# Two graph attention layers: both normalisations and the ELU's minimum on VectorE, half of the maxima subtracted inside the exponent, and a new order on every engine

## The reference

```python
q, k, v = x @ Wq + bq, x @ Wk + bk, x @ Wv + bv          # layer 0, 6 heads
probs = softmax(q @ k.T / sqrt(64) + where(adj, 0, NEG))
x = layernorm(x + (probs @ v) @ Wf + bf)
h = einsum('bnd,ade->bane', x, W)                        # layer 1, 12 heads
attn = tanh(h) @ w_src + (tanh(h) @ w_dst).T
attn = softmax(where(adj, leaky_relu(attn, 0.2), -999))
f = elu(attn @ h + b)
gate = sigmoid(x @ H_w.T + H_b)
out = layernorm(x + gate * f + (1 - gate) * x)
```

## Time and profile before

| | |
|---|---|
| median of 3 runs | 1220.42 us (1217.51 to 1220.64) |
| profiled execution | 1217.34 us, its span 1215.6 us |
| granted TensorE clock, mean | 0.974 |
| busy | PE 90%, PEld 80%, DVE 79%, ACT 80%, POOL 82% of the span |
| DMA engines | 31.2% |

### The profile page before, as it was taken

One profiled execution on the slowest core, in us unless ns is written; L12 is line 12 of the kernel. 1 busy time (PEld: TensorE's weight loads), 2 busy tenths in 40 slices (PEclk: granted clock), 3 DMA queues, 4 the chain that ended last, 5 costly groups with the idle time before them and its releaser, 6 DMA issues.

```text
span 1215.6 us, 35318 instructions
## 1 busy us (share of the span) xinstructions
PE 1091.1 (90%) x12234; PEld 975.3 (80%) x12297; DVE 962.6 (79%) x1948; ACT 968.6 (80%) x1868; POOL 1000.1 (82%) x813
## 2 busy tenths in 40 slices
PE   4689999999999999999999999999999999999851
PEld 4578888888888888888888888888888888888741
DVE  5567888888888888888888888888888888888843
ACT  5258888888888888888888888888888888888854
POOL 1138898888989888889988888988888898988876
PEclk9799999999999999999999999999999999999975
DMA  4103332223333222333322233332223333223233
GB/s 144 43 17 83 81 90 65 73 68 93 87 86 92 66 68 67 93 87 87 93 66 66 68 93 89 85 93 66 66 74 87 93 87 86 73 67 75 68 66 79
DMA packets 244762, 95.18 MB, mean 78 GB/s; under 512 B 223349, under 2 KB 239738, under 8 KB 244730
## 3 DMA queue, kind: packets, MB, share of 16 engines
q1 hardware_dynamic: 244730, 94.76, 31.2%
HBM read 31.22 MB, written 12.58 MB: 36 GB/s over the span
## 4 chain that ended last, share of the span: by engine, by line
PE 56%; POOL 15%; issue 14%; DVE 11%; ACT 2%; DMA 1%; DVEq 1%; SPq 0%; POOLq 0%; ACTq 0%
PE lin L448 33%; PE zp L545 6%; POOL z L1295 5%; POOL prod L1254 5%; PE fp L570 3%; PE zp L603 3%; PE zp L607 3%; DVE sd L978 2%; PE fp L620 2%; PE fp L573 2%; PE tp L487 2%; DVE y L1073 1%; DVE f L1117 1%; DVE z L1098 1%; ACT th L721 1%
## 5 line engine op out<-in xcount | busy, mean ns | idle before, releaser
L1302 POOL TENSOR_TENSOR p_lo<-z,p_hi 128x1536 f16<-128x1536 f32 x64 | 200.9, 3139 | 0.0
L1295 POOL TENSOR_TENSOR z<-z,z_max 128x1536 f32<-128x1536 f32 x64 | 176.5, 2758 | 9.1 <-DVE z_max L1105 6.1
L784 ACT ACTIVATE z<-zp 128x1536 f32<-128x1536 f32 x64 | 93.1, 1455 | 85.9 <-PE zp L607 85.9
L1254 POOL TENSOR_TENSOR prod<-th,w_sd_rows 128x768 f32<-128x768 f32 x64 | 120.5, 1883 | 14.0 <-ACT th L721 14.0
L620 PE MATMUL fp<-h_part,p1t_hi 128*128 128x33 bf16 x2304 | 110.6, 178 | 19.2 <-DMA p1t_lo<-p_lo 14.8
L620 PEld LDWEIGHTS fp<-h_part,p1t_hi 128*128 128x128 f16 x2304 | 104.4, 96 | 27.2 <-issue 24.1
L1307 POOL TENSOR_TENSOR f<-f,x_kept 128x384 f32<-128x384 f32 x64 | 64.7, 1011 | 73.6 <-DVE f L1124 69.4
L1098 DVE SCALAR_TENSOR_TENSOR z<-zp,z 128x1536 f32<-128x1536 f32 x64 | 112.2, 1753 | 11.0 <-ACT z L784 8.3
L776 ACT ACTIVATE p<-p,p_min 128x128 f32<-128x128 f32 x384 | 118.9, 396 | 0.0
L1105 DVE TENSOR_REDUCE z_max<-z 128x12 f32<-128x1536 f32 x64 | 111.6, 1744 | 0.0
L623 PE MATMUL fp<-h_part,p1t_lo 128*128 128x33 bf16 x1536 | 106.8, 178 | 0.0
(11 more groups left out here) (161 smaller groups left out, 4387.0 us busy)
## 6 DMA issues: line engine op xcount, KB each, us to landing
xt_raw<-x_t SPq DMA_DIRECT2D x32, 384.0 KB, 3.4
x_raw<-x SPq DMA_DIRECT2D x32, 384.0 KB, 3.5
out<-out_tile SPq DMA_DIRECT2D x64, 192.0 KB, 1.9
adj<-adj SPq DMA_DIRECT2D x64, 32.0 KB, 2.8
dst_row<-sd_t SPq DMA_DIRECT2D x64, 9.0 KB
p1t_hi<-p_hi SPq DMA_TRANSPOSE x64, 3.3
p1t_lo<-p_lo SPq DMA_TRANSPOSE x64, 3.3
z<-Wq SPq DMA_DIRECT2D x1, 576.0 KB, 3.5
```

The lines of the kernel that those rows point to most:

```text
L784: act.activation(z[:, g, :], zp[:, :, :].rearrange("p b n -> p (b n)"), ACT.Copy)\
L1254: pool.tensor_tensor(prod[:, g, :].rearrange("p (s d) -> p s d", s=2), th[:, g:g + 1, :].to_broadcast([128, 2, D]), rows["w_sd"][:, :].rea ...
L1295: pool.tensor_tensor(zs, zs, z_max[:, g, :].unsqueeze(2).to_broadcast([128, H1, N]), ALU.subtract)\
L1302: pool.tensor_tensor(p1_lo[:, g, :], z[:, g, :], p1_hi[:, g, :], ALU.subtract).then_inc(w1_lo[g].sem, 1)
```

## The change

Four things, and with them new orders on all five engines:
- The two normalisations move from ScalarE to VectorE, as one tensor_scalar each, (y - mean) x rstd; the two shifts go.
- The ELU's Relu on ScalarE becomes min(f, 1) on VectorE; the exponent takes the bias -1.
- GpSimd subtracts the maxima of heads 0 to 5 alone. For heads 6 to 11 VectorE makes an offset log(PSCALE) - max (`z_shift`, 12 columns), and ScalarE takes one exponent per head with that offset as the bias.
- The lists of steps are new, and with them the users' order of the PSUM banks `tp` and `fp`.

```diff
+SUBTRACTED = 6
...
-                def norm0(g):
-                    act.wait_ge(norm0_shift[g].sem, now(norm0_shift[g]))
...
-                    act.activation(x1[:, g, :], y[:, g, :], ACT.Identity, bias=shift0[:, g, :], scale=rstd[:, g, :])\
-                        .then_inc(x1_ready[g].sem, 1)
                 def z_exponent(g):
+                    act.wait_ge(z_offsets[g].sem, now(z_offsets[g]))
+                    for h in range(SUBTRACTED, H1):
+                        act.activation(z[:, g, N * h:N * (h + 1)], z[:, g, N * h:N * (h + 1)], ACT.Exp,
+                                       bias=z_offset[:, g, h:h + 1])
                     act.wait_ge(z_sub[g].sem, now(z_sub[g]))
-                    act.activation(z[:, g, :], z[:, g, :], ACT.Exp, bias=log_scale[:, :]).then_inc(z_exp[g].sem, 1)
+                    act.activation(z[:, g, 0:SUBTRACTED * N], z[:, g, 0:SUBTRACTED * N], ACT.Exp, bias=log_scale[:, :])\
+                        .then_inc(z_exp[g].sem, 1)
...
-                def shift_norm0(g):
+                def norm0(g):
                     dve.wait_ge(y_rstd[g].sem, now(y_rstd[g]))
...
+                    dve.wait_ge(x1t_mm[g].sem, now(x1t_mm[g]))
+                    dve.wait_ge(x1_copied[g].sem, now(x1_copied[g]))
+                    dve.tensor_scalar(x1[:, g, :], y[:, g, :], moments[:, g, 0:1], rstd[:, g, :],
+                                      ALU.subtract, ALU.mult).then_inc(x1_ready[g].sem, 1)
...
+                def z_shift(g):
+                    dve.wait_ge(z_maxed[g].sem, now(z_maxed[g]))
+
+                    dve.wait_ge(z_exp[g].sem, prev(z_exp[g]))
+                    dve.tensor_scalar(z_offset[:, g, :], z_max[:, g, :], -1.0, math.log(PSCALE), ALU.mult, ALU.add)\
+                        .then_inc(z_offsets[g].sem, 1)
...
+                def features_negative(g):
+
+                    dve.wait_ge(f_norm[g].sem, now(f_norm[g]))
+                    dve.wait_ge(f_elu[g].sem, prev(f_elu[g]))
+                    dve.tensor_scalar(f_neg[:, g, :], f[:, g, :], 1.0, None, ALU.min).then_inc(f_min[g].sem, 1)
...
-                def shift_norm1(g):
+                def norm1(g):
...
+                    dve.tensor_scalar(out_tile[:, g, :], y2[:, g, :], moments2[:, g, 0:1], rstd2[:, g, :],
+                                      ALU.subtract, ALU.mult).then_inc(out_ready[g].sem, 1)
...
-                    zs = z[:, g, :].rearrange("p (a n) -> p a n", a=H1)
+                    zs = z[:, g, 0:SUBTRACTED * N].rearrange("p (a n) -> p a n", a=SUBTRACTED)
...
                 turn.late(0, context_transposes, 1)
+                turn.late(1, attention1, 1)
                 turn.late(0, project, 0)
-                turn.late(1, attention1, 1)
...
                 turn.step(1, x1_transposes, 0)
+                turn.step(1, x1_transposes, 1)
                 turn.step(0, values, 1)
```

More of the change, by code:

```diff
@@ L647, in body @@
                 turn.step(1, hidden, 0)
-                turn.step(1, x1_transposes, 1)
                 turn.step(0, scores, 1)
+                turn.step(1, hidden, 1)
                 turn.step(2, attend1, 0, 0)
-                turn.step(1, hidden, 1)
-                turn.step(0, weights0_transposes, 0, 0)
                 turn.step(2, attend1, 0, 1)
                 turn.step(2, attend1, 0, 2)
+                turn.step(0, weights0_transposes, 0, 0)
                 turn.step(1, gate_rows, 0)
[L656 to L659, removed]
             turns(pe, passed, body)
@@ L815, in weights1_high @@
                     act.activation(p1_hi[:, g, :], z[:, g, :], ACT.Copy).then_inc(w1_hi[g].sem, 1)
[L817 to L822, removed]
                 def elu_exp(g):
                     act.wait_ge(f_min[g].sem, now(f_min[g]))
[L826 to L833, removed]
+                    act.activation(f_neg[:, g, :], f_neg[:, g, :], ACT.Exp, bias=minus_one[:, :])\
+                        .then_inc(f_exp[g].sem, 1)
                 def next_x_high():
@@ L860, in body @@
                 turn.step(0, value_part1, 1)
-                turn.step(0, value_part2, 0)
-                turn.late(0, norm0, 1)
-                turn.step(-1, next_x_high)
[L864 to L868, removed]
-                turn.step(0, weights0_high, 0, 0)
[L870 to L889, removed]
+                turn.step(1, x1_high, 1)
+                turn.late(1, gate_quarter, 1)
+                turn.late(1, hidden_part2, 1)
+                turn.step(1, hidden_tanh, 0)
+                turn.step(0, scores_exp, 0)
+                turn.step(1, hidden_tanh, 1)
+                turn.step(-1, next_x_high)
+                turn.step(0, weights0_high, 0, 0)
             turns(act, passed, body, other_weights)
@@ L906, in _ @@
             dve.memset(dst_row[:, :, :, :], 0.0)
-            dve.memset(one[:, :], 1.0)
+            dve.memset(minus_one[:, :], -1.0)
             dve.memset(log_scale[:, :], math.log(PSCALE))
@@ L1165, in body @@
+                turn.late(2, moments1, 0)
                 turn.late(0, moments0, 1)
+                turn.late(0, variance0, 0)
+                turn.late(0, variance0, 1)
+                turn.late(2, variance1, 0)
                 turn.step(0, value_residue, 0)
+                turn.late(0, norm0, 0)
+                turn.late(2, stats1, 1)
+                turn.late(0, norm0, 1)
                 turn.step(0, queries_keys, 1)
-                turn.late(2, moments1, 0)
-                turn.late(2, variance1, 0)
@@ L1191, in body @@
                 turn.step(1, source_target_part2)
+                turn.step(1, source_target_part3)
+                turn.step(2, features_negative, 0)
                 turn.late(2, variance1, 1)
-                turn.step(1, source_target_part3)
-                turn.step(2, elu, 0)
                 turn.step(0, weights0_low, 0, 1)
@@ L1198, in body @@
                 turn.step(1, hidden_raised, 1)
+                turn.step(0, weights0_low, 1, 0)
                 turn.step(0, weights0_low, 1, 1)
-                turn.step(0, weights0_low, 1, 0)
                 turn.step(0, context_inverse, 0)
                 turn.step(0, context_norm, 0)
-                turn.late(2, shift_norm1, 1)
+                turn.step(2, elu, 0)
+                turn.step(2, features_negative, 1)
+                turn.late(2, norm1, 1)
                 turn.step(0, context_inverse, 1)
+                turn.step(0, context_norm, 1)
+                turn.step(1, z_leak, 0)
+                turn.step(0, context_low, 0)
+                turn.step(1, z_maxima, 0)
+                turn.step(2, elu, 1)
+                turn.step(1, z_shift, 0)
+                turn.step(0, context_low, 1)
             turns(dve, passed, body, other_weights)
```

126 lines of the change are left out of this document (64 added, 62 removed).

## The result

The changed kernel takes 1291.09 us in the median of 4 runs (1289.99 to 1291.88), the kernel before 1219.49 (1217.51 to 1220.64): ratio 1.0588, 95% interval 1.057 to 1.0607. It is 72 us slower; forecast were 1298, in a range from 1200 to 1342. One turn, measured at the transposes of sd_parts over 20 turns, takes 37.70 us and took 35.33.

What follows compares the result with a forecast made beforehand. TensorE sets the pace, busy 33.52 of a 35.34 us turn, with VectorE making it wait. Holds +3.05 and order -0.5 gave +2.55 per turn, x 31 = +79, so 1298 us, range 1200 to 1342.

Steps and rivals of the forecast that it cites:

- The hold: VectorE operations needing the second SBUF path stand still until GpSimd's whole instruction ends; losses sum to +3.05 us per turn.
- norm0(1): Layer 0 normalisation of graph 1 on VectorE: held 2.8 us by weights1_low(0), slack 1.0, TensorE loses about 1.7 per turn.
- norm1(0): Second normalisation of graph 0 on VectorE: held 2.4 us by weights1_low(1), loss 0.75 before scores(1).
- norm1(1): Second normalisation of graph 1, behind elu(0) and the minimum: held about 0.9 us by features_difference, loss 0.6.
- z_shift(1): VectorE's offset, waiting for the same maxima as z_subtract(1): counted 0, with 1.4 us of hold kept for the range.
- The order, -0.5 per turn: New lists without holds: shorter TensorE waits against +0.45 us at queries_keys(1), sum -0.5 per turn, -15 us.
- The waits of project(0) and values(0): TensorE's 0.40 us wait for ctx_lo goes; 0.3 of the 0.41 wait for y goes.
- the 0.45 at the transposes of sd_parts: TensorE's wait for VectorE there: the sd chain begins about 0.5 us earlier, so 0.25 of it goes.
- The new wait of 0.45 at queries_keys(1) for gate_tanh(1): On ScalarE gate_tanh(1) stands behind z_exponent(0) and weights1_high(0); TensorE needs the bank it frees, +0.45 us.
- Sum: Holds +3.05 less 0.5 for the order: +2.55 us per turn, x 31 = +79.
- No hold: Rival: one-input tensor_scalar with pointer scalars does not take GpSimd's path; the order's gain stands, 1205 us; chance 0.23.
- dissolve: Rival: holds exist, but held VectorE work shifts until it falls into GpSimd's idle time; 1210 to 1250 us; chance 0.10.

Runs made afterwards that it cites:

- e1: Small separate kernel without the computation, timing single VectorE forms alone and beside GpSimd; 384-column tensor_scalar with pointer scalars 0.48 us alone, held to GpSimd's end.
- e11: Changed kernel with the destinations of VectorE's two normalisations in rows of 128 columns and 4 unused, no wait or order changed; 1209.58 us.
- e13: e11 with PSUM banks exchanged, VectorE's low parts ahead of elu and residual, and ScalarE's gate_tanh(1) ahead of weights1_high(0); 1251.30 us.
- e6: e3 with attention1(1) on TensorE put back between project(0) and project(1), as in the kernel before; 1270.40 us.
- e2: Changed kernel with one wait more: GpSimd's weights1_low(0) waits until norm0(1) is written; 1243.39 us.
- e3: Changed kernel with GpSimd's weights1_low(0) waiting for norm0(1), weights1_low(1) for norm1(0), and norm1(1) ahead of elu(0) on VectorE; 1233.98 us.
- e12: Kernel before with its own lists, both normalisations and the minimum moved to VectorE, their destinations in rows with gaps; 1285.99 us.
- e5: Changed kernel with norm0, norm1(0) and the minima (as Relu) back on ScalarE, norm1(1) on VectorE ahead of elu(0); 1258.69 us.

## Why the prediction was right, step by step

- **The hold** (two-path operations of VectorE stand still for GpSimd's whole instruction): right. e1 shows it by itself and e11 shows its price: without it 1209.6 us instead of 1291.1, a turn of 34.95 instead of 37.70, so 2.75 us. Predicted were 3.05. TensorE's idle time is 2.07 of the 2.75, just what the waits below add up to; the other 0.68 is time in which it counts as busy, and no run shows what lengthens it. The Trainium skill ("SBUF — State Buffer", Who interferes with whom) states this exclusion; the 2.93 us of norm0(1) and the 0.66 of e11 agree.
- **norm0(1)**: hold predicted 2.8, measured 2.45 (2.93 - 0.48), since the normalisation itself takes 0.48, not 0.35, and starts 0.42 into GpSimd's instruction, not 0.27. Loss predicted 1.7 (my own 2.8 less 1.0 is 1.8), measured 0.97 at x1_transposes and 0.24 at values(1), in all 1.2. The place and the second waiter were right, the slack was 1.24 instead of my 1.0.
- **norm1(0)**: hold 2.4, measured 2.3; loss 0.75, measured 0.61 at scores(1). **norm1(1)**: hold 0.9, measured 0.7; loss 0.6, measured 0.26 ahead of attention1. **z_shift(1)** counted nothing, and costs nothing: it starts 0.05 ahead. e1 holds such an operation for 2.90 us and e13 this very one for 0.45, so that is a matter of who comes first, not of its width. That it came first was counted on without a row that showed it, and was luck.
- **The order, -0.5 per turn**: the sum was near, its parts were not. e11, the new order without holds, has a turn of 34.95, 0.38 below the 35.33 of before. But only about 0.05 of that is idle time of TensorE; the rest is busy time (33.20 us per turn instead of 33.54, over ten turns of each), which the prediction did not count. The waits of project(0) and values(0) are gone as said. Of the 0.45 at the transposes of sd_parts 0.09 is gone, not 0.25. The new wait of 0.45 at queries_keys(1) for gate_tanh(1) does not exist: attention1(1), earlier now, lets ScalarE copy z earlier. In its place stand two that I had not seen: 0.30 for sd_t behind the transposes of sd_parts, and 0.94 at project(1): with attention1(1) gone from between them, both projects use one bank back to back. e6 shows the two bound together: with attention1(1) back, the wait for y goes from project(1) and that for gate_tanh(1) comes.
- **Sum**: predicted +2.55 per turn, measured +2.37. The waits of the turn shown, 1.2 + 0.61 + 0.26 + 0.94 + 0.30 = 3.3, less 0.9 of gone ones and of two small ones more in the kernel before (0.22 for f, 0.17 that no releaser explains), give 2.0, the growth of TensorE's idle time; the other 0.35 is busy time. Counted by waits the three hold terms were too large by 1 us (2.1 against 3.05), and what made it up were waits and busy time that the prediction did not have. So the closeness of 1298 to 1291 is partly luck.
- **The rivals.** "No hold" falls; its 1205 is what e11 reaches (1209.6) once the hold is taken away. Holds do move: in e2 and e3 the minimum took over part of them. But in the changed kernel they did not dissolve by themselves.

## What to carry to other kernels

Before moving work to VectorE next to a busy GpSimd, ask of each operation whether it needs VectorE's second path (one input at double rate, or two inputs, in SBUF) and what GpSimd runs when it starts; its length then is GpSimd's, not its own. If it meets a long instruction on the critical chain, a layout that forbids the double rate costs 0.2 us and saved 2.3 here (norm0(1), 2.93 to 0.66). And where an idle spell of TensorE is followed by half clock, as in e12, price the wait with the clock's loss behind it.

## What the runs showed of the hardware

- A tensor_scalar of 384 float32 columns in SBUF takes 0.36 us with a constant and 0.48 with two pointer scalars; from PSUM 0.68 and with gaps on one side 0.67, both with pointers (0.55 with gaps and a constant, the minimum of e12). I had expected no price for the pointers.
- 12 columns are held to GpSimd's end like 384 (2.90 and 3.08 us); one column is not held (0.15).
- GpSimd can be the one that waits: at 533.87 in the changed kernel the minimum (0.35) and GpSimd's part of the values start together, and GpSimd's takes 1.12 us. At the same place in e5, which has no minimum on VectorE, it takes 0.89.
- The even and the odd columns in turn (a step of two elements on both sides) run at the same 0.36 and 0.48 us as contiguous ones, and are held alike.
- In e12 a wait of 1.08 us, in place of 0.45, was followed in every turn by about 4 us at a granted clock of 0.5 to 0.6. In e11 and the changed kernel waits of 0.94 us at project(1), and in the changed kernel one of 0.97 at x1_transposes, were followed by none, so the length of the wait alone does not decide it.
